# Cross-attention with sparsemax and a cosine/sine ffn on one core: row sums first in a phase, attention work between steps of the projections, corrections as one loop

## The reference, cut to what matters

```python
x = x + xattn(layernorm(x), ctx_1024)        # x: 8 x 100 x 512, ctx: 8 x 722 x 512
x = x + ffn(layernorm(x))
# xattn, 16 heads of 32:
scores = einsum('bhqd,bhkd->bhqk', qh, kh) * scale
attn = sparsemax(scores)                     # clip(scores - tau, 0): every row sums to 1
out = einsum('bhqk,bhkd->bhqd', attn, vh)    # then @ Wo + bo
# ffn: sqrt((x @ cos(theta + theta_noise))**2 + (x @ sin(phi + phi_noise))**2)
```

## Time and profile before

| | |
|---|---|
| median of 3 runs | 919.28 us (918.03 to 923.22) |
| profiled execution, its own time | 921.24 us |
| its span, first to last instruction | 919.5 us |
| mean granted TensorE clock | 0.752 of full speed |
| busy: PE, DVE, ACT, POOL | 75%, 57%, 53%, 22% of the span |

### The profile page before, as it was taken

One profiled execution on the slowest core, in us unless ns is written; L12 is line 12 of the kernel. 1 busy time (PEld: TensorE's weight loads), 2 busy tenths in 40 slices (PEclk: granted clock), 3 DMA queues, 4 the chain that ended last, 5 costly groups with the idle time before them and its releaser, 6 DMA issues.

```text
span 919.5 us, 13912 instructions
## 1 busy us (share of the span) xinstructions
PE 687.3 (75%) x4528; PEld 406.0 (44%) x4528; DVE 528.4 (57%) x2366; ACT 488.1 (53%) x925; POOL 203.3 (22%) x242
## 2 busy tenths in 40 slices
PE   4679393786956969697888879797396978886474
PEld 2345162542634436463555436463264635452241
DVE  5999892751937539434746539434684348365500
ACT  4445465464544655646565646655266455554631
POOL 4454221041130411222040402221022220301201
PEclk9788677597685986778695976788567786957857
DMA  9630202002030020202020020203002020200000
GB/s 325 207 87 29 73 15 68 2 16 84 4 88 2 17 84 11 81 1 70 31 66 27 25 76 18 75 1 99 2 17 77 1 58 3 59 1 9 11 1 9
DMA packets 33484, 44.36 MB, mean 48 GB/s; under 512 B 8347, under 2 KB 26779, under 8 KB 33376
## 3 DMA queue, kind: packets, MB, share of 16 engines
q1 hardware_dynamic: 32320, 41.09, 15.4%
q10 hardware_dynamic: 1056, 2.10, 0.7%
HBM read 23.77 MB, written 1.64 MB: 28 GB/s over the span
## 4 chain that ended last, share of the span: by engine, by line
PE 50%; ACT 16%; issue 16%; DVE 13%; DVEq 2%; DMA 1%; SPq 1%; POOL 1%; ACTq 0%; POOLq 0%
PE ring L454 21%; PE ring L592 7%; PE mix_bank L565 6%; PE ring L520 6%; PE ring L540 4%; ACT S L775 4%; ACT S L669 3%; PE ring L493 3%; DVE cand L934 3%; ACT pT L796 2%; PE ring L505 2%; ACT qst L669 2%; DMA v<-in_L_ffn_theta_noise 1%; ACT ks L677 1%; DVEq L1034 1%
## 5 line engine op out<-in xcount | busy, mean ns | idle before, releaser
L934 DVE MAX8 cand<-S 100x8 f32<-100x60 f32 (+1 forms) x1536 | 191.1, 205 | 0.1
L669 ACT ACTIVATE S<-ring 100x722 f32<-100x722 f32 x128 | 95.0, 772 | 145.8 <-DVEq L1041 105.9
L540 PE MATMUL ring<-kst,qst 96*100 96x361 f16 x256 | 80.2, 433 | 110.4 <-ACT S L669 93.9
L454 PE MATMUL ring<-wv,ctx 128*121 128x512 f16 x576 | 144.1, 403 | 0.0
L454 PE MATMUL ring<-ctx,wk 128*128 128x361 f16 x768 | 136.4, 343 | 4.9 <-DVE ctx L1076 4.9
L796 ACT ACTIVATE pT<-ring 121x800 f32<-121x800 f32 x96 | 80.2, 838 | 77.0 <-PE ring L592 77.0
L775 ACT ACTIVATE S<-S,neg_tau 100x722 f32<-100x722 f32 x128 | 114.3, 903 | 2.7 <-DVE neg_tau L970 2.7
L592 PE MATMUL ring<-qst,kst 99*121 99x100 f16 x768 | 96.2, 304 | 20.4 <-ACT qst L669 20.4
L454 PEld LDWEIGHTS ring<-ctx,wk 128*128 128x128 f16 x768 | 81.2, 106 | 62.1 <-issue 16.8
L338 POOL TENSOR_TENSOR ks<-k_f,ks 128x361 f16<-128x361 f32 x64 | 62.9, 983 | 190.8 <-ACT k_f L681 189.0
L454 PEld LDWEIGHTS ring<-wv,ctx 128*121 128x121 f16 x576 | 83.2, 144 | 47.9 <-issue 7.5
(11 more groups left out here) (121 smaller groups left out, 780.5 us busy)
## 6 DMA issues: line engine op xcount, KB each, us to landing
kst<-ks SPq DMA_DIRECT2D x384, 45.1 KB, 1.9
ctx_f<-in_ctx SPq DMA_DIRECT2D x45, 242.0 KB, 2.9
xq<-in_x SPq DMA_DIRECT2D x8, 200.0 KB
xr<-in_x SPq DMA_DIRECT2D x8, 200.0 KB
out_y<-att SPq DMA_DIRECT2D x8, 200.0 KB
S<-in_L_xattn_Wk ACTq DMA_DIRECT2D x1, 1024.0 KB, 6.8
wq<-in_L_xattn_Wq ACTq DMA_DIRECT2D x1, 1024.0 KB, 11.8
wcos<-in_L_ffn_theta SPq DMA_DIRECT2D x1, 1024.0 KB, 10.5
```

What stands on the lines that cost most here:

```text
L454: last = nc.tensor.matmul(psum, lhs(c, i), w(c, j), start=(c == 0 and n == 0), stop=(c == DC - 1 and n == 2))
L540: last = nc.tensor.matmul(psum[0:L, half, 0:HALF], qst[0:3 * DH, b % 2, HH * part + h, :], kst[0:3 * DH, i % 3, h, half * HALF:(half + 1) ...
L669: return nc.scalar.activation(dst, src, ACT.Copy, **kw)
L934: last = nc.vector.max(cand[:, h, 8 * n:8 * n + 8], S[0:L, HH * (i % 2) + h, cuts[n]:cuts[n + 1]])
```

## The change

Three edits. In each phase the row sums now stand right behind the K reads on ACT, and the flags right behind K on PE. The attention of part i - 1 then comes before any score of part i + 1, and one step of V (even phases) or of transposed x, queries and ffn (odd phases) is put behind each of its 13 steps; the scores come last, with what is left of the fill between them. On DVE `settle(i - 1)` stands after the seventh head of `maxes(i)`, and its corrections are one loop over the heads with the head in a register, with one flag word loaded in each pass.

```diff
                 if odd:
...
+                    if attended:
+                        sum_flags(i - 1)
+                    ffn = ffn_of(b - 1) if 0 <= b - 1 < B else iter(())
+                    fill = chain(*([xT_of(b + 1)] if 0 <= b and b + 1 < B else []),
+                                 *([q_of(b + 1)] if b + 1 < B else [iter([None] * 6)]), ffn)
+                    for _ in units:
+                        run(fill, 1)
+                    run(fill, 5 if b < 0 else 0)
                     if b + 1 < B:
                         run(transpose_q(b + 1), 2)
-                    run(early, 2)
+                    weave(heads, fill, 1)
+                else:
...
                     if attended:
                         sum_flags(i - 1)
+                    fill = chain(*[v_of(b, kc) for kc in range(KC)]) if b < B else iter(())
                     run(fill, 4)
-                    run(early, 2)
-                    run(units, 15)
-                    run(late, 4)
...
+                    for _ in units:
+                        run(fill, 1)
+                    weave(heads, fill, 1)
                     if b > 0:
                         run(o_of(b - 1), 4)
```

ACT, odd phases (even ones alike, with `root` and V pieces between the units):

```diff
+                    for half in range(2):
+                        for m in range(2):
+                            if b + 1 < B:
+                                k_of(b + 1, m, half)
+                            run(checks, 3)
+                    run(units, 1)
+                    if 0 <= b and b + 1 < B:
+                        xT_of(b + 1)
+                    run(units, 2)
                     if 0 <= b - 1 < B:
                         ln_sd(b - 1, mv2, sd2, ln2_stat, ln2_sd)
+                    run(units, 1)
                     if b + 1 < B:
                         q_of(b + 1)
+                    run(units, 1)
                     if 0 <= b - 1 < B:
                         x2T_of(b - 1)
+                    run(units, 2)
```

DVE:

```diff
-                todo = dve.value_load(flag_i[0:1, 0:1], min_val=0, max_val=2 ** HH - 1)
+                todo = dve.value_load(any_i[0:1, 0:1], min_val=0, max_val=1)
                 with dve.If(todo > 0):
                     dve.wait_ge(tau_split, i + 1)
-                    for h in range(HH):
-                        with dve.If((todo >> h) & 1 > 0):
+                    with dve.Fori(0, HH) as h:
+                        rows = dve.value_load(flag_i[0:1, bass.ds(h, 1)], min_val=0, max_val=1)
+                        with dve.If(rows > 0):
                             refine(i, h)
                     split_again(i)
...
                     found = maxes(i, h)
-                    if h == 1 and odd and b >= 1:
+                    if h == 6 and i > 0:
+                        settle(i - 1)
+                    if h == 4 and odd and b >= 1:
                         ln2_stats(b - 1)
-                    if h == 4 and odd and b >= 1:
+                    if h == 6 and odd and b >= 1:
                         ln2_apply(b - 1)
```

More of the change, by code:

```diff
@@ L110, in build_kernel @@
                     use(two, ("st", i - 1, g, c))
-        for h in range(G, HH):
+        if odd and b + 1 < B:
+            use(two, ("qT", b + 1, 0))
+            use(two, ("qT", b + 1, 1))
+        for h in range(HH):
             if i + 1 < NH:
@@ L616, in _ @@
                 attended, scored = 0 <= i - 1 < NH, i + 1 < NH
-                early = scores(i + 1, range(G)) if scored else iter(())
-                late = scores(i + 1, range(G, HH)) if scored else iter(())
                 units = attend(i - 1) if attended else iter(())
+                heads = scores(i + 1, range(HH)) if scored else iter(())
                 if odd:
@@ L623, in _ @@
                     if b + 1 < B:
[L624 to L631, removed]
+                        run(k_of(b + 1, 0, 0), 4)
+                        run(k_of(b + 1, 1, 0), 4)
@@ L815, in _ @@
                 attended, scored = 0 <= i - 1 < NH, i + 1 < NH
-                checks = check(i - 1) if attended else iter(())
+                units, checks = (attend(i - 1), check(i - 1)) if attended else (iter(()), iter(()))
                 if odd:
@@ L844, in _ @@
-                    if scored:
-                        for h in range(G):
+                    for h in range(HH):
+                        if scored:
                             score(i + 1, h)
-                            if h == 2 and 0 <= b - 1 < B:
-                                square(b - 1, 1)
-                    elif 0 <= b - 1 < B:
-                        square(b - 1, 1)
-                    if attended:
-                        attend(i - 1)
-                    if scored:
-                        for h in range(G, HH):
-                            score(i + 1, h)
-                else:
-                    if b < B:
-                        k_of(b, 2, 0)
-                        k_of(b, 2, 1)
+                        if h == 3 and 0 <= b - 1 < B:
+                            square(b - 1, 1)
+                else:
+                    for m in (2, 3):
+                        for half in range(2):
+                            if b < B:
+                                k_of(b, m, half)
+                            run(checks, 3)
@@ L936, in maxes, with thresholds @@
                 return counted(last)
-            def thresholds(i, found, between):
+            def thresholds(i, found):
                 t = neg_tau[:, i % 2, :]
@@ L946, in thresholds @@
                 for turn, ranks in enumerate(RANKS):
-                    if turn == 1:
-                        between()
                     E = PIECES * ranks
@@ L1112, in _ @@
                         ln1_stats(b + 1)
-                thresholds(i, found, lambda: settle(i - 1) if i > 0 else None)
+                thresholds(i, found)
                 if not odd and b + 1 < B:
```

107 lines of the change are left out of this document (39 added, 68 removed).

## The result

The changed kernel takes **864.96 us** in the median of 4 runs (863.91 to 869.06), beside 918.75 for the kernel before: a ratio of 0.941, with an interval of 0.938 to 0.945. The profiled execution has a span of 862.8 us at a mean clock of 0.829; before 919.5 at 0.752.

The account below looks back on a forecast made before the run. PE leads the chain, slowed by the wait for `verified` and a low clock (0.752 mean). Start 121, six phase pairs 546.6, corrections 52, phase 14 46.6 and end 81 sum to 847 us; range 822 to 905.

Parts of the forecast that it names:

- Up to the flags: Start of both kinds of phase: flags 12.4 us behind the start of K, PE idle 4.9 us in every phase.
- The settle: DVE's check behind the flags: its jump passes 57 instructions, not 366, so `verified` comes 1.3 us behind the flags, not 4.1.
- The gap that it named as a sign: DVE's "issue" gap behind the settle's load: near 0.3 us instead of 3.97.
- Rival 1: Corrections' loop on DVE: each jump back is a fetch, 39 to 71 us more, 886 to 918, or near 880; chance 0.17.
- The first 5 us run at half clock, 2.5 more: Odd phases behind `verified`: half clock for 5 us adds 2.5 to 26.7 and PE's 1.4 wait, making the phase 44.5.
- Rival 2: Odd phases: the clock stays low without a dense V piece, about 57 us each; 935, or 891 if in half; chance 0.13.
- In even phases 4.2 of it lie behind V: 16.4 twice and 19.3 once: Three corrected parts: each correction costs 20.6 us, V hides 4.2 of it in even phases; 52 us in all.
- Even phases: Plain even phases: 46.6 us each, before 52.1; V piece 4.2, waits for ACT 1.3, K's half clock 1.7 included.
- The start: Phases 0 and 1: phase 1 begins some 4 us later, then gains 10 to 12; phase 2 starts at 121, 6 earlier.
- Mean clock: Sign over the whole kernel: a mean clock of 0.85 or more, where it was 0.752.
- Rival 3: Handovers to ACT, or a jump of 57 still costing 3.4, lengthen phases by 1.5 to 3 us: 868 to 890; chance 0.13.
- Rival 4: Low clock holds in even phases too: even phases reach 61, odd 57 us, kernel slower at 1020 to 1035; chance 0.05.

Follow-up runs that it names:

- e3: The changed kernel with the attention in one piece and its fill behind it, not interleaved; 931.02 us, ratio 1.012 to the kernel before.
- e2: The changed kernel with the corrections as eight unrolled copies again, new order and place of the settle kept; 865.94 us, ratio 0.943.
- e1: The kernel before with only the corrections made one loop over the heads, at their old place; 897.04 us, ratio 0.974.
- e7: The changed kernel with transposed x and queries ahead of the flags in odd phases, ACT's copies placed to suit; 822.81 us, ratio 0.895.
- e8: The changed kernel with the two Sin activations of phase 2 moved ahead of its attention, behind the first V copy; 861.36 us, ratio 0.936.
- e9: The changed kernel with a bound so low that no head is flagged, so no corrections run; 807.53 us, ratio 0.880.
- e4: The kernel before with only the settle moved on DVE, to after the seventh head of the maxima; 917.49 us, ratio 0.997.
- e13: e11 with the eight unrolled copies of the corrections in place of the loop; 831.14 us, ratio 0.905.
- e11: The changed kernel with the edits of e7 and e8, and even phases' first V piece ahead of the flags; 800.68 us, ratio 0.872.

## Why the prediction was right, and where it was off

The sign holds, and the time is 18 us above the 847, inside the range. Of the two mechanisms the first holds: attention at full clock behind interleaved work (e3 loses 66 us without it). The second, a shorter settle, came about, but the time does not come from it: e2 has the long one and is as fast (865.94). By its own sum:

```
term                        predicted   measured   difference
start of phase 2              121         120.1       -1
6 even phases, plain          46.6 each   46.1        -3
6 odd phases, plain           44.5 each   46.0        +9
corrections                   52          62.6       +10.6
phase 14                      46.6        45.4        -1
from phase 15's start         81          82.1        +1
sum                           847         862.8 (span)
```

(Measured: the means of the plain phases; for the corrections what phases 2, 4 and 11 have over those means; phase 15 begins at 780.75, where PE falls idle for 8.05 us ahead of the flags at 788.80.)

**Up to the flags**: right. They come 12.26 us behind the start of K, predicted 12.4 (the terms that it names make 12.1); PE stands idle 4.72, predicted 4.9. Only where K starts at half clock is it later.

**The settle**: 1.3 predicted behind the flags, 1.55 to 1.92 measured from the flags to the thresholds on PE, against 4.1 to 4.5 with the jump over 366 instructions (e2). The gap that it named as a sign, near 0.3, is 1.3 to 1.6 on DVE in plain parts; less the 0.5 of the load, a jump over 57 costs some 0.8, where 0.14 to 0.5 was taken (and by these terms the sign should have been 0.7 to 1.0, not 0.3). What failed in the reasoning is the step from a shorter settle to a shorter phase: odd phases 7, 9 and 13 are as long with the long settle, with 2.6 us more idle and 2.8 less busy time of PE (e2). The Trainium skill ("Runtime: NRT & Kernel Launch", "Instruction fetch mechanics") has a taken branch stall when its target is not in the two blocks of 256 instructions at hand. The traces agree in part: twelve jumps over 366 left gaps of 3.53 to 4.74 us (the kernel before), twelve over 57 gaps of 1.02 to 1.63 (nine in e1, three in the changed kernel). By the page's figures, as an estimate, a jump over 366 that begins early in the first of the two blocks would end in the second and not stall; none of the twelve was short. Rival 1, a fetch in each pass of the loop, did not come: the three corrected settles lie within 0.6 us of each other (21.90 to 22.48), and in the settle of part 10 the two gaps of 8.96 and 4.81 us, less five loads of 0.3 that are outside of the loop's own, hold all eight passes, that is at most 1.5 us for a pass, where 1.2 was counted and a fetch in each would have made it 2.8 or more. The rows on DVE:

```profile
598.77 0.91 DVE L961 TENSOR_SCALAR_CACHE_REDUCE over<-S 100x722 bf16 x1 [8.96 <-issue]
...
609.78 0.17 DVE L1001 TENSOR_SCALAR t_rest<-neg_tau 100x8 f32<-100x8 f32 x1 [4.81 <-remote]
```

**Odd phases, 1.5 us short each.** The step is "The first 5 us run at half clock, 2.5 more". The low clock lasted 7 us behind the thresholds (498.93 to 506), and it came a second time, 3.5 us long, behind the wait for ACT's copy. The wait itself was priced rightly (1.4, measured 1.36); what I did not price is what it does to the clock. 5.5 us more at half clock are at most 2.7 of time, so the rest of the walk was about 1 us a phase too dear, and the two errors cancel in part. Rival 2 was so partly true: odd phases run at 0.84, even ones at 0.90. e7 fills PE's idle stretch and takes the wait for the copy out, and with it the second fall of the clock; one low stretch is left (0.87). That gives 6 us a phase.

**Corrections, the term that was furthest off.** The step is "In even phases 4.2 of it lie behind V: 16.4 twice and 19.3 once". Several things were off. The Sin activations and their table load, 5 us on ACT, lay before in ACT's wait for `verified`, 105.9 us in all; I took the wait away and did not ask what it had covered (the rows of e8). e8 gives 5.5 of phase 2 back and 3.6 of the whole. The others are size: 19.1, 19.2 and 20.5 us over the same phase in e9, where 16.4, 16.4 and 19.3 stood. The settle of part 10 was 1.3 longer than the 20.6 (21.9 from flags to thresholds on PE), that of part 3 was 22.5. And the clock falls through it (0.73 to 0.79 in these phases).

**Even phases**: right within 0.5, in part because errors cancel. The V piece took 5.38 at half clock where 4.2 was taken; PE's idle time outside of the wait for the flags was 1.0 in the whole phase, where 1.3 was predicted for ACT inside the attention alone.

**The start**: right to 1 us, in phase 0 (4.5 us longer, predicted 4) and in phase 1 (11.1 shorter, predicted 10 to 12). It gave phase 1's gain to the place of the settle, and e4 has only 4.7 of it from there. The loop alone (e1) takes 4.0 off phase 1, and order and place without the loop (e2) 6.2. So the size was right and its cause in part: here the shorter settle does count. The place alone, over the whole kernel, gives 2.

**Mean clock**: 0.85 or more predicted, 0.829 measured. Without the corrections it is 0.852.

**Rival 3** (handovers, or a jump of 57 that still costs 3.4) did not come: the jump costs some 0.8, and PE waits little for ACT inside the attention.

**Rival 4** did not come as named, but e3 shows its ground: with the flags first and no dense work between the units, the kernel is slower than before.

What stays open is why the clock returns when it does. The worth of the loop (22, 1, 30) depends on it in e2, by the busy times; in e13 some 6 of the 30 us are in no trace, since the executions profiled lie closer than the medians. No run here sets the clock while it holds the work fixed.

## What to carry to other kernels

When a wait is removed or shortened, list what ran under it on every engine: here two Sin activations of 5 us that no one had paid for came onto the path. The worth of one part (the loop) was 22, 1 and 30 us in three orders of the same work, so try a part again when what hid it has moved. After a change of order, split a phase into PE's busy and idle time before naming a cause: here the wait that was to go was replaced by another as long, and the gain was the clock. And fill the idle stretch that is left: 4.7 us of it in odd phases, filled with work that was there anyway, gave 42 us beside the 54 of the whole change, most of it idle time and some of it clock.

## What the runs showed of the hardware

In these traces small matmuls that kept PE busy did not bring the full clock back, but kept it where it was up: in e3 a block of st and mix ran at 0.50 in phase 8 (its PE rows without a gap from 496.72 to 505.79) and at full speed in phases 6 and 12. In e11, four even phases of the same instructions took 42.3, 43.8, 45.8 and 44.6 us in one execution, with a granted clock of 0.96, 0.92, 0.89 and 0.89: differences of 3 us between phases need not have a cause in the program. And 2.4 us more of waiting cost nothing in phases 7, 9 and 13 of e2: the half clock ended at about the same distance from K, and PE needed 33.2 busy us instead of 36.0 for the same work.
